# Attention tiles whose projection, fourth norm and ternary product move from behind the loop into it

## The reference, cut to what matters

```python
x = x + xattn0(layernorm(x)); x = x + ffn0(layernorm(x))
# third block: N = 1024 queries, 1024 keys, H = 16, hd = 16
q = fq(layernorm(x) @ Wq + bq); k, v = fq(ctx @ Wkv + bkv)
attn = fq_unsigned(softmax(q @ k.T / 4))
x = x + (attn @ v) @ Wp + bp
# fourth block
x = x + layernorm(x) @ ternary(weight).T + bias
```

## Time and profile before

| | us |
|---|---|
| three executions | 337.09, 335.58, 336.85 (median 336.85) |
| profiled execution, its own time | 337.5 |
| span of the profile | 335.7 |
| stages in front of the loop | 0 to 129.1 |
| attention loop, first exp to end of last exp | 129.1 to 302.4 (173.3) |
| behind the loop | 302.4 to 335.7 (33.3) |

### The profile page before, as it was taken

How to read it: one execution, slowest core, us unless ns; L and a number is a source line. 1 busy time by engine, 2 the same in 40 slices (tenths; PEclk the granted TensorE clock), 3 DMA queues, 4 the chain that set the end, 5 groups by cost and what they waited for, 6 DMA issues and landing times.

```text
span 335.7 us, 5142 instructions
## 1 busy us (share of the span) xinstructions
PE 268.7 (80%) x1728; PEld 127.3 (38%) x1728; DVE 265.7 (79%) x401; ACT 210.0 (63%) x340; POOL 98.3 (29%) x225
## 2 busy tenths in 40 slices
PE   4993597595156947899999999999999999979670
PEld 4441365473034733233333332333333333338560
DVE  3363799968697878999999899899999999973850
ACT  1100125435533178999999999999999999992210
POOL 2350424476603011221222212222222122211634
PEclk9999559987555977555555555555555555558998
DMA  7824000039100001999999999999999999995011
GB/s 255 276 94 126 0 3 0 0 59 161 34 0 0 0 2 37 196 182 206 185 200 178 215 172 212 184 212 164 227 167 219 197 188 190 199 184 109 16 49 63
DMA packets 148618, 43.34 MB, mean 129 GB/s; under 512 B 143216, under 2 KB 147696, under 8 KB 148592
## 3 DMA queue, kind: packets, MB, share of 16 engines
q1 hardware_dynamic: 146496, 39.60, 65.4%
q0 software_dynamic: 768, 2.10, 1.8%
q10 hardware_dynamic: 1328, 1.32, 1.2%
HBM read 5.25 MB, written 2.10 MB: 22 GB/s over the span
## 4 chain that ended last, share of the span: by engine, by line
issue 36%; DVE 18%; PE 17%; POOL 16%; ACT 6%; DMA 6%; POOLq 1%; ACTq 0%; DVEq 0%
POOL ebias L421 8%; PE ps L1175 5%; PE ps L1158 4%; PE ps L1047 3%; DMA ksplit<-in_x 3%; DVE nmax L878 2%; ACT ctxT L566 2%; POOL scratch L369 2%; PE ps L1150 2%; POOL rstd L375 2%; POOL xs L432 2%; DMA xs<-scratch 2%; POOL out L446 1%; DVE stats L850 1%; ACT kv L557 1%
## 5 line engine op out<-in xcount | busy, mean ns | idle before, releaser
L878 DVE TENSOR_REDUCE nmax<-ps 128x1 f32<-128x1024 f32 x128 | 156.3, 1224 | 16.5 <-PE ps L1175 11.6
L1175 PE MATMUL ps<-keysT,kv 64*128 64x512 bf16 x256 | 130.1, 614 | 9.2 <-ACT ctx L566 1.9
L566 ACT ACTIVATE ctx<-ps,ebias,qscale 128x1024 int16<-128x1024 f32 x64 | 76.9, 1203 | 5.4 <-POOL ebias L421 3.5
L566 ACT ACTIVATE ctxT<-ps,ebias,qscale 128x1024 int16<-128x1024 f32 x64 | 77.0, 1203 | 4.0 <-POOL ebias L421 2.5
L1204 PEld LDWEIGHTS ps<-vals,ksplit 128*128 128x128 f16 x1024 | 36.9, 105 | 100.6 <-issue 100.3
L421 POOL TENSOR_SCALAR ebias<-nmax,qcur 128x1 f32<-128x1 f32 x128 | 33.8, 264 | 136.2 <-DVE nmax L878 127.2
L1204 PE MATMUL ps<-vals,ksplit 128*128 128x16 f16 x1024 | 47.7, 176 | 0.8 <-DVE krest L923 0.8
L475 ACT COPY hT<-ps 128x256 f32<-128x256 f32 x11 | 4.1, 372 | 46.5 <-PE ps L1039 46.5
L1175 PEld LDWEIGHTS ps<-keysT,kv 64*128 64x128 bf16 x256 | 16.3, 107 | 21.8 <-ACT ctx L566 8.1
L543 ACT COPY hT<-ps 128x512 f32<-128x512 f32 x8 | 4.7, 586 | 22.5 <-PE ps L1150 22.5
L1022 PE MATMUL ps<-wkv_s,ctxT 128*128 128x512 f32 x32 | 16.4, 668 | 0.7 <-ACT ctxT L469 0.7
(11 more groups left out here) (176 smaller groups left out, 316.1 us busy)
## 6 DMA issues: line engine op xcount, KB each, us to landing
ctx<-in_ctx SPq DMA_DIRECT2D x2, 512.0 KB, 4.9
ksplit<-in_x ACTq DMA_DIRECT2D x1, 1024.0 KB, 10.9
xs<-scratch SPq DMA_DIRECT2D x1, 1024.0 KB, 5.6
wkv_s<-in_L_xattn_Wkv SPq DMA_DIRECT2D x1, 512.0 KB, 8.1
ksplit<-ctx SPq DMA_TRANSPOSE x32, 4.7
ksplit<-ctxT SPq DMA_TRANSPOSE x32, 4.9
bkv_b<-in_L_xattn_bkv ACTq DMA_DIRECT2D x1, 256.0 KB, 11.4
wt_s<-in_L_ffn_weight SPq DMA_DIRECT2D x1, 256.0 KB, 9.4
```

The source lines that it names most:

```text
L566: a.activation(prob_of(w)[:, (u % 2) * NK:(u % 2 + 1) * NK], score_banks(k, u), ACT.Exp, bias=ebias[:, u % 4:u % 4 + 1], scale=qscale[:, t ...
L878: v.tensor_reduce(nmax[:, u % 4:u % 4 + 1], score_banks(k, u), AX.X, ALU.max, negate=True).then_inc(max_ready, 1)
L1175: last = m.matmul(ps[:, bank + b, :], qT[rows, t, u // 2, :], keysT[rows, u // 2, 512 * b:512 * b + 512], start=True, stop=True)
```

## The change

What stood behind the loop is done inside it, tile by tile, for all but the last tiles. In tile t PE transposes the attention result of tile t-1 after head 9 and multiplies it by Wp after head 11; after head 4 it transposes the normed rows of tile t-2 and after head 6 it multiplies them by the ternary weights. ACT copies both transposes to SBUF (after heads 10 and 5). DVE adds the projection (after head 14), takes the sums (after head 15) and adds the ternary product (after head 9). POOL computes the inverse root (after head 1), norms in two halves of 128x128 (after heads 2 and 3) and issues the scatter (after head 12). The biases bp and bt are no longer added by POOL and DVE: a matmul of one row (ones by bias, 256 columns) opens each product. To make room in PSUM, the weighed values of all tiles use bank 6 and the new work bank 7; the first weigh of a tile moves from head 6 to head 7, where two weighs stand. The copy `qcur` is gone.

```diff
-        PV_BANKS = [6, 7, 6]
+        PV_BANK = 6
+        FINISH = 7
...
+        def finish_turn(t):
+            return ps[:, 0, 0:D] if t == NT - 1 else ps[:, FINISH, D:2 * D]
+        def finish_product(t):
+            return ps[:, 1, 0:D] if t == NT - 1 else ps[:, FINISH, 0:D]
...
         @block.gpsimd
...
             def attention(t, k):
-                if not first_tile(t):
-                    pool.wait_ge(bias_ready, t * H)
-                g.tensor_copy(qcur[:, :], qscale[:, t, :]).then_inc(qcur_ready, 1)
-                pool.wait_ge(qcur_ready, t + 1)
                 for u in range(H):
                     exp_bias(t, u)
-                    if u == H // 2:
-                        g.tensor_tensor(xs[:, t, :], xs[:, t, :], bp_b[:, :], ALU.add).then_inc(x3b_ready, 1)
+                    if t >= 2:
+                        if u == 1:
+                            fourth_root(t - 2)
+                        if u in (2, 3):
+                            fourth_norm(t - 2, u - 2)
+                        if u == 12:
+                            scatter_output(t - 2)
+            def fourth_root(t):
+                pool.wait_ge(sums4_ready, t + 1)
+                inverse_root(t, t + 1, rstd4)
+                pool.wait_ge(rstd4, t + 1)
+            def fourth_norm(t, c):
+                g.tensor_scalar(hs[:, t, c * P:(c + 1) * P], xs[:, t, c * P:(c + 1) * P], mv[:, t, 0:1], rstd[:, t:t + 1],
+                                ALU.subtract, ALU.mult).then_inc(h4_ready, 1)
...
         @block.scalar
...
             def attention(t, k):
                 for u in range(H):
                     head_exp(t, k, u)
+                    if u == 5 and t >= 2:
+                        copy_h4(t - 2)
+                    if u == 10 and t >= 1:
+                        copy_att(t - 1)
...
         @block.vector
...
+                    if u == DIVIDE_AT + 1 and t >= 2:
+                        add_ternary(t - 2)
+                    if u == H - 2 and not first_tile(t):
+                        add_projection(t - 1)
+                    if u == H - 1 and not first_tile(t):
+                        fourth_sums(t - 1)
...
         @block.tensor
...
+            def product_tile(lhs, w, bias, t, out, full):
+                m.matmul(out, onesf[0:1, :], bias[0:1, :], start=True, stop=False)
+                for c in range(C):
+                    last = m.matmul(out, lhs[:, t % 2, c, :], w[:, c, :], start=False, stop=(c == C - 1))
+                last.then_inc(full, 1)
...
-                    if u >= WEIGH_LAG:
+                    if u == WEIGH_LAG + 1:
+                        weigh(t, k, 0)
+                    if u > WEIGH_LAG:
                         weigh(t, k, u - WEIGH_LAG)
-                    elif not first_tile(t):
+                    elif u < WEIGH_LAG and not first_tile(t):
                         weigh(t - 1, k - 1, u - WEIGH_LAG + H)
+                    if t >= 2:
+                        if u == 4:
+                            h4_turn(t - 2)
+                        if u == 6:
+                            ternary(t - 2)
+                    if t >= 1:
+                        if u == 9:
+                            att_turn(t - 1)
+                        if u == 11:
+                            project(t - 1)
```

More of the change, by code:

```diff
@@ L420, in exp_bias @@
                 slot = slice(u % 4, u % 4 + 1)
[L421 removed]
+                g.tensor_scalar(ebias[:, slot], nmax[:, slot], qscale[:, t, u:u + 1], LN255,
                                 ALU.mult, ALU.add).then_inc(bias_ready, 1)
             def attention(t, k):
[L425 to L427 removed]
@@ L435, in _ @@
             pool.wait_ge(qinv_ready, 2)
             tiles(pool, attention)
[L438 to L456, removed]
+            fourth_root(NT - 2)
+            for c in range(C):
+                fourth_norm(NT - 2, c)
+            scatter_output(NT - 2)
+            fourth_root(NT - 1)
+            for c in range(C):
+                fourth_norm(NT - 1, c)
@@ L457, in _ @@
+            scatter_output(NT - 1)
             pool.wait_ge(stored, 16 * NT)
@@ L1197, in weigh @@
                 pair_turned(pe, t, u // 2)
-                if u == 0 and k % NS == 0 and not first_tile(t):
+                if u == 0 and not first_tile(t):
                     pe.wait_ge(att_ready, t)
-                if u == 0 and k % NS == 2:
-                    pe.wait_ge(att_ready, t - 1)
-                out = ps[:, PV_BANKS[k % NS], u * HD:(u + 1) * HD]
+                out = ps[:, PV_BANK, u * HD:(u + 1) * HD]
                 for r in range(KT):
@@ L1206, in weigh, with turn_tile, att_turn, project @@
                 last.then_inc(pv_done, 1)
+            def turn_tile(src, t, out, full):
+                for c in range(C):
+                    last = m.transpose(out[:, c * P:(c + 1) * P], src[:, t, c * P:(c + 1) * P], identf[:, :])
+                last.then_inc(full, 1)
+            def product_tile(lhs, w, bias, t, out, full):
+                m.matmul(out, onesf[0:1, :], bias[0:1, :], start=True, stop=False)
+                for c in range(C):
+                    last = m.matmul(out, lhs[:, t % 2, c, :], w[:, c, :], start=False, stop=(c == C - 1))
+                last.then_inc(full, 1)
+            def att_turn(t):
+                pe.wait_ge(att_ready, t + 1)
+                if 1 <= t < NT - 1:
+                    pe.wait_ge(x4_ready, t)
+                turn_tile(att, t, finish_turn(t), attT_full)
+            def project(t):
+                pe.wait_ge(attT_ready, t + 1)
+                product_tile(attT, wp_s, bp_b, t, finish_product(t), proj_full)
+            def h4_turn(t):
+                pe.wait_ge(h4_ready, C * (t + 1))
+                turn_tile(hs, t, finish_turn4(t), h4T_full)
+            def ternary(t):
+                pe.wait_ge(h4T_ready, t + 1)
+                product_tile(hT, wtT, bt_b, t, finish_product4(t), tern_full)
             def attention(t, k):
@@ L1242, in late_weigh @@
                 weigh(NT - 1, NT - 1, u)
-            pe.wait_ge(exp_done, NT * H)
-            for g in range(3):
-                att_turn(g)
-            pe.wait_ge(scaled_wp, 1)
-            project(0)
             for u in range(H - WEIGH_LAG, H - 2):
                 late_weigh(u)
-            project(1)
-            pe.wait_ge(att_ready, NT - 1)
-            project(2)
+            h4_turn(NT - 2)
+            ternary(NT - 2)
             late_weigh(H - 2)
             late_weigh(H - 1)
-            h4_turn(0)
-            ternary(0)
-            h4_turn(1)
-            att_turn(3)
-            project(3)
-            ternary(1)
-            h4_turn(2)
-            h4_turn(3)
-            ternary(2)
-            ternary(3)
+            att_turn(NT - 1)
+            project(NT - 1)
+            h4_turn(NT - 1)
+            ternary(NT - 1)
 _NAMES = ["x", "itok_BxS_13_99985", "ctx_2048", "L0_ffn_weight", "L1_xattn_Wq", "L1_xattn_bq", "L1_xattn_Wkv",
```

95 lines of the change are left out of this document (41 added, 54 removed).

## The result

The changed kernel takes **377.81 us** (376.88 to 379.27, four runs), against 336.87 for the kernel before beside it: a ratio of 1.1228, with a 95% interval of 1.1181 to 1.1276. It is slower by 12%. The forecast was 366.5 with a range of 350 to 376: the direction was right, and the time lies 1.8 us outside the range.

The account below looks back on a forecast made before the run. It took the loop to be bound by its round's latency across four engines, TensorE 5% behind. From 335.7 us of span, +41.4 in the loop and -11.8 behind it gave 365.3, forecast as 366.5 us, range 350 to 376.

Parts of the forecast that it names:

- Clock at 0.50 through the loop: Main forecast: TensorE's clock stays at 0.50 in nearly all of the loop, 366.5 us; chance 0.62.
- A: Rival: the clock rises around the products in the loop, saving 11.7 us there and 2.5 behind it, 352 us; chance 0.25.
- B: Rival: full clock through the loop from tile 1 on, VectorE the bound, about 22.2 us a tile, 326 us; chance 0.06.
- Turn and copy, 1.07 less 0.2 of slack: Each transpose with its copy costs PE 1.07 us (0.42 work, 0.65 idle), less 0.2 already idle in a round.
- A product, 1.71 us for two wide f32 matmuls and 0.85 for the bias: PE's price per product in the loop at half clock: 1.71 us, plus 0.85 for the bias matmul unless hidden.
- I count the ternary's bias as hidden beside those scores: After head 6 the one-row bias runs beside head 9's scores on the other row half, free; otherwise 5.1 us more.
- The base of a tile: Loop tile before the new work: bound by its round's latency, 16 x 1.343 = 21.5 of 21.7 us measured.
- The sums: VectorE's sums after head 15 delay the next maximum by 0.55 us in 6 tiles: 3.3 us.
- VectorE's additions, GpSimd's root, norms and scatter in the loop at nothing: In the loop the additions hide behind PE's products and GpSimd's work fits: 0 taken, 5.4 us kept for the range.
- Behind the loop, 21.5 us: From the last exp's end to the end: 33.3 us falls to 21.5, a gain of 11.8 us.
- Rival C: More waits in the loop: bias not hidden (5.1) and GpSimd's root and scatter delaying rounds (5.4), 377 us; chance 0.07.
- The own range of the forecast: 361 to 372 us: copies' idle half covered (4.2 less, 1 for the tail) or the bias not hidden (5.1 more).

Follow-up runs that it names:

- Experiment 2: Changed kernel with the bias product made of 128 rows (1/128 in every row of the left side) in place of one row: 369.27 us, ratio 1.0987.
- experiment 6: Kernel before, with four unread bf16 matmuls of 128 rows by 256 columns ahead of each weigh: 426.0 us, ratio 1.2596.
- experiment 3: Changed kernel with both copies, both products and both additions one head later: 371.05 us, ratio 1.1016.
- experiment 1: Changed kernel without the one-row bias products (both biases left out): 361.19 us, ratio 1.0728.
- experiment 4: Changed kernel with the sums of the fourth norm directly behind the addition of the projection: 376.42 us, ratio 1.1185.
- experiment 5: Changed kernel with both products and their one-row biases in bf16, transposes still f32: 342.92 us, ratio 1.0123.
- experiment 7: Changed kernel with four unread full-row bf16 matmuls ahead of each weigh: no steady time, 372.67 to 405.97 us, median 400.95.

## What the prediction had right, and the steps that made it too low

**Clock at 0.50 through the loop, forecast 0.62 against A and B:** right. It fell at 129.9 and did not rise in 246 us. Experiment 2 shows how near rival A was: with 128 rows in the bias product the clock does rise behind a product, ten times. The argument against A in the prediction (an expert stage that stayed at 0.50) gave the right answer, but the rows of the one-row product, which decided, were not in it. By the rule of the Trainium skill in "TensorE: Matmul & The Clock Gate" (Part 1: The HAM clock gate), that activity releases the throttle, the loop should have run at the high clock; it is 94% busy and stands at 0.50 throughout, so the trace disagrees again. The last sentence of the prediction has the low state rest on the 64-row scores; experiment 6 stayed low with full-row products between them, so what it rests on is open.

**Turn and copy, 1.07 less 0.2 of slack:** 0.98 measured for each (1.96 in a tile). Right, and experiment 3 shows its idle half: 6.8 us of the forecast 13 x 0.65 = 8.5. (Two slips in this part of the sum cancel: 1.07 + 1.71 - 0.2 is 2.58 and not 2.55, 1.07 + 2.56 - 0.2 is 3.43 and not 3.45. And PE's 1.28 splits into 0.96 for scores and 0.32 for a weigh, not 0.85 and 0.43; the sum does not hang on it.)

**A product, 1.71 us for two wide f32 matmuls and 0.85 for the bias:** this term was mis-sized. The rows have 2.01 and 1.14. The four records of the wide product take 4 x 0.43 here as in the expert stage; what is new is 0.28 behind the bias and 0.29 behind the wide pair, until the next instruction starts; with 128 rows (experiment 2) it was 0.14 and 0.12. The price was read where one f32 product follows another, and used where it stands between bf16 scores. Thirteen times 0.59 is 7.7 us. Each record's weight load shows 0.33 us in the changed kernel, and two of the scores' 0.13, so an exposed load is the likely filling of that gap. The timelines bear it out for the gap behind the bias: behind the one-row product the first load of the wide pair starts with the pair (216.84, changed kernel), behind the full-row one 0.43 ahead of it (308.30 and 308.73, experiment 2):

```profile
216.84 1.35 PEld L1232 LDWEIGHTS ps<-wtT,hT 128*128 128x128 f32 x4 [0.65 <-issue]
```

```profile
308.30 1.62 PEld L1234 LDWEIGHTS ps<-wp_s,attT 128*128 128x128 f32 x4
308.73 1.91 PE L1234 MATMUL ps<-wp_s,attT 128*128 128x256 f32 x4
```

No experiment changed the load alone, and for the gap behind the wide pair it is argued only.

**"I count the ternary's bias as hidden beside those scores":** this step failed. The one-row product starts 0.96 after the scores, the distance of any other instruction, and experiment 1 finds no free one in the full tiles. Two row halves at work together had been seen for two bf16 scores; it did not carry over to an f32 product of one row behind them. The Trainium skill, in "TensorE: Matmul & The Clock Gate" (Part 3: Packing small matmuls), has matmuls in different row groups run at the same time; the trace does not agree for this pair, which starts 0.96 us apart. Which of the differences (type, rows, the neighbour's two matmuls) forbids it was not tried. Six times 0.85 is 5.1 us, the bound that the prediction itself had worked out.

**The base of a tile:** PE now bounds it but for one round of 4.04, so that it is 16 x 1.28 and 0.2, 20.7, and not the 21.7 - 0.16 - 0.4 = 21.1 that was left of the latency round. This gives back 0.4 a tile. **The sums:** 0.64 of waits where 0.55 was forecast; experiment 4 took 0.34 of it away, in five tiles of six.

**VectorE's additions, GpSimd's root, norms and scatter in the loop at nothing:** right. The additions have PE's product as cover (waits of 1.93 ahead of them). GpSimd has 55 us of work in 224; its norm takes 0.80, twice the upper bound that had been taken from a copy of twice the width, and still fits.

By the terms a tile is 1.9 more for the products, 0.4 less for its base and 0.1 less for the rest: 28.1 + 1.4 = 29.5, the measured one. Six such tiles and a seventh projection make 8.8 of the 9.6 by which the loop was underestimated.

**Behind the loop, 21.5 us:** 24.9. Of the 3.4, about 1.1 is the last two products (3.3 each from the copy's end on, where 2.75 was counted), 0.95 the last norm, 0.8 the part at high clock that had been counted on and did not come, 0.4 the scatter; the rest is small.

**Rival C, 377 us,** came out at the right number by luck, for half of its reasons: the bias not hidden (5.1) is in the trace, the waits behind GpSimd (5.4) are not, and the longer products, which it did not have, fill their place. The own range of the forecast held the bias not hidden, but not together with a longer product: both errors were in the price of the same product, and both ran the same way.

**Where the cost came from at all:** 34.9 of 41 us go with the type of the products (experiment 5), 6.8 with the place of the copy (3), 1.7 with the sums (4, by its timeline). With these three taken out the loop still is longer than before (186.7 us against 173.3), and the shorter tail (19.2 against 33.3) pays for it: 336.1 against 338.1, level.

The type is not the only way to read the price. The kernel before had the same wide f32 products, all behind the loop, where the clock was at 1.00 from 305.3 on the earlier trace rows, and no bias product (group by form: busy us, mean ns, idle before):

```profile
L1158 PE MATMUL ps<-wp_s,attT 128*128 128x256 f32 x32 | 7.7, 388 | 0.7 <-ACT attT L543 0.7
L1158 PE MATMUL ps<-wtT,hT 128*128 128x256 f32 x32 | 7.5, 381 | 0.8 <-ACT hT L543 0.8
```

That is 15.2 us for 16 products, 0.95 each. In the changed kernel the same 16 take 2.01 each and 1.14 for the bias, 50.4 us. So PE is given 17 us more for the same wide products, by the half clock and the new neighbours, and 18 for the bias products, which replaced additions on GpSimd and VectorE. The prediction had the half clock in its prices (1.71 us for a wide pair); the neighbours it had not.

## What to carry to other kernels

A price for a matmul has to be read between the neighbours that it will have: two f32 matmuls took 2.0 us between bf16 scores where they had taken 1.7 among their like, and a one-row matmul cost more than a full-row one. Work moved out of a serial tail into a loop is free only on an engine that has the time at the clock that the loop runs at; here the tail gave 8.4 us and the loop took 51.0, because PE had 1.2 us free in a tile and was handed 7.5 (two products of 3.15, two transposes of 0.60), at half the clock at which it had done this work in the tail. If such a move is made, make the work short first (bf16: 34.9 us), and then put an engine's consumer one step behind its producer (6.8 us).

## What the runs showed of the hardware

- A one-row f32 product of 256 columns took 1.14 us at clock 0.50, one of 128 rows 1.00; the wide pair behind it took 2.01 and 1.84.
- With the full-row bias the clock came up ten times, each time for about 3.4 us; with the one-row bias never. A loop 94% busy (208.4 of 221.0 us) at half clock did not bring it up, nor did one filled with full-row bf16 products in experiment 6 (258.0 of 258.0 us busy), while the same fills in experiment 7 brought it for 47 us at a stretch.
- GpSimd's subtract-and-multiply of 128x128 with two values per row took 0.80 us (16 of them, 0.78 to 0.81); VectorE did 128x256 in 0.41.
- A GpSimd result reached VectorE 0.48 us after its end, where GpSimd's own next instruction followed after 0.11.
